# Weighted sums of a graph-attention layer: the product with the coefficients moves from GpSimd to VectorE, and the loads change order

## The reference, cut to what matters

```
x = leaky(x, 0.01) @ W1.T + b1
h = (x @ Wg.T).reshape(N, H, C)
...
coeff = ex / (denom[dst] + 1e-16)
msg = h[src] * coeff[:, :, None]
out = jax.ops.segment_sum(msg, dst, num_segments=N)
out = out.reshape(N, H * C) + bias_g
out = leaky(out, 0.01) @ W2.T + b2
```

## Time and profile before

| | us |
|---|---|
| median of 3 executions | 3251.99 (3251.73 to 3252.8) |
| the profiled execution, its own time | 3261.0 |
| its span, first to last instruction | 3259.2 |
| weighted sums, first load issued to barrier | 1563.3 to 1731.3 |
| busy in the span: TensorE, VectorE, ScalarE, GpSimd | 1741.0, 1931.8, 1077.7, 2424.7 |
| mean granted TensorE clock, share of full speed | 0.671 |

### The profile page before, as it was taken

One profiled execution on the slowest core, in us unless ns is written; L12 is line 12 of the kernel. 1 busy time (PEld: TensorE's weight loads), 2 busy tenths in 40 slices (PEclk: granted clock), 3 DMA queues, 4 the chain that ended last, 5 costly groups with the idle time before them and its releaser, 6 DMA issues.

```text
span 3259.2 us, 39190 instructions
## 1 busy us (share of the span) xinstructions
PE 1741.0 (53%) x7779; PEld 1286.0 (39%) x7779; DVE 1931.8 (59%) x6186; ACT 1077.7 (33%) x2956; POOL 2424.7 (74%) x2038
## 2 busy tenths in 40 slices
PE   1442005888803555563683335667667746555553
PEld 1342004777701222221462334445445535455553
DVE  6984446887813555555896775333333367666664
ACT  1321004665603444442354554222222222212110
POOL 4776787788887777771466775888888878888887
PEclk9665557988956766666555556676676667666666
DMA  8899995455642333331573554565666555555554
GB/s 185 240 311 358 337 354 158 69 61 84 116 36 61 80 79 80 80 79 42 173 217 98 130 131 114 114 116 110 115 114 109 117 124 125 116 114 110 115 114 73
DMA packets 423456, 436.97 MB, mean 134 GB/s; under 512 B 55330, under 2 KB 348883, under 8 KB 423061
## 3 DMA queue, kind: packets, MB, share of 16 engines
q0 software_dynamic: 128576, 130.98, 26.1%
q1 hardware_dynamic: 237472, 240.03, 24.1%
q10 hardware_dynamic: 57336, 65.24, 7.2%
HBM read 248.75 MB, written 187.31 MB: 134 GB/s over the span
## 4 chain that ended last, share of the span: by engine, by line
POOL 29%; issue 12%; DVE 5%; PE 3%; ACT 2%; DMA 1%; ACTq 1%; DVEq 0%; SPq 0%; POOLq 0%
POOL out_dram L718 19%; POOL work L704 11%; DVE work L2103 2%; PE bank L937 1%; ACT work L1322 1%; PE bank L1032 1%; DVE work L1907 1%; PE bank L1110 0%; DMA work<-he,idx_last_s 0%; ACT work L1423 0%; PE bank L1096 0%; DVE work L2140 0%; DVE work L2141 0%; DVE work L2139 0%; DMA work<-s,idx_e_d 0%
## 5 line engine op out<-in xcount | busy, mean ns | idle before, releaser
L1907 DVE TENSOR_TENSOR_SCAN work<-work,bank 128x512 f32<-128x512 bf16 (+1 forms) x294 | 364.1, 1264 | 316.4 <-PE bank L937 292.0
L718 POOL DMA_INDIRECT out_dram<-work,idx_add_s x196 | 313.0, 1597 | 64.7 <-issue 58.5
L718 POOL DMA_INDIRECT out_dram<-big,idx_add_d x196 | 314.8, 1606 | 60.2 <-issue 58.8
L718 POOL DMA_INDIRECT out_dram<-big,idx_add_s x196 | 310.5, 1584 | 61.5 <-issue 54.5
L1315 ACT ACTIVATE work<-work,eps_col 128x4 f32<-128x4 f32 (+1 forms) x196 | 58.5, 299 | 718.0 <-DVE work L1883 717.5
L704 POOL DMA_INDIRECT big<-x_by_edge,idx_e_s x196 | 220.1, 1123 | 75.3 <-issue 59.4
L937 PE MATMUL bank<-ident,work 128*128 128x128 f32 x392 | 106.0, 424 | 298.2 <-ACT work L1322 170.8
L996 PE MATMUL bank<-ident,work 128*128 128x128 f32 x392 | 91.8, 411 | 309.9 <-ACT work L1322 309.9
L1322 ACT ACTIVATE work<-work 128x128 f32<-128x128 f32 x588 | 236.7, 480 | 50.9 <-DVE work L1902 50.9
L704 POOL DMA_INDIRECT work<-he,idx_last_s x196 | 191.4, 977 | 75.5 <-issue 59.4
L704 POOL DMA_INDIRECT work<-d,idx_run_d x196 | 187.6, 957 | 75.4 <-issue 59.4
(11 more groups left out here) (362 smaller groups left out, 5396.7 us busy)
## 6 DMA issues: line engine op xcount, KB each, us to landing
out_dram<-work SPq DMA_DIRECT2D x57, 726.0 KB, 9.0
work<-in_x_dram SPq DMA_DIRECT2D x57, 704.0 KB, 10.1
edge_w<-work SPq DMA_DIRECT2D x49, 512.0 KB
work<-edge_w ACTq DMA_DIRECT2D x49, 512.0 KB, 3.7
work<-flags_src SPq DMA_DIRECT2D x98, 128.0 KB
gat_h<-work SPq DMA_DIRECT2D x49, 256.0 KB
work<-flags_dst SPq DMA_DIRECT2D x98, 128.0 KB
work<-gat_h SPq DMA_DIRECT2D x49, 256.0 KB
```

Of the source, the lines that this page charges most:

```text
L718: g_.indirect_dma_start(table[:, :], bass.IndirectOffsetOnAxis(ap=of[:, at_:at_ + 1], axis=0), row, None, compute_op=ALU.add).then_inc(add ...
L1907: return V.tensor_tensor_scan(to, flag_b[G.place][rows, :], of, before if G.from_(1) else 0.0, ALU.mult, ALU.add)
```

## The change

The GpSimd product and the ScalarE copy before it are taken out. VectorE now multiplies `in_r` by the spread coefficients straight from the PSUM bank. VectorE's body becomes product(G), scan(G-1), leaky(G-2), so scan and leaky each stand one body later than before, and one scan and two leakys follow after the loop. TensorE's spread waits for the product of G-2 (which read its bank) where it waited for the copy. SyncE's order of the three loads becomes coefficients, `gat_h`, flags. The semaphore `coef` is gone.

```diff
             def body(G):
-                load_flags(sp, G, "dst", GATSUM)
+                load_coefficients(sp, G)
                 if G.from_(UNROLL):
                     sp.wait_ge(GATSUM["h"], G.g - (UNROLL - 1))
                     plain(sp)
                 sp.dma_start(in_r[G.place], at(h_dram, G, 512)).then_inc(h_in.of(G), 16)
-                load_coefficients(sp, G)
+                load_flags(sp, G, "dst", GATSUM)
...
-            def products(G):
-                pool.wait_ge(GATSUM["coef"], G.g + 1)
-                h_in.wait(pool, "GATSUM", G)
-                if G.from_(2):
-                    pool.wait_ge(GATSUM["chained"], G.g - 1)
-                g_.tensor_tensor(h_r[G.slot], in_r[G.place], co_r[G.place], ALU.mult).then_inc(GATSUM["h"], 1)
-            for_groups(pool, products)
...
             def spread(G):
                 h_in.wait(pe, "GATSUM", G)
                 if G.from_(2):
-                    pe.wait_ge(GATSUM["coef"], G.g - 1)
+                    pe.wait_ge(GATSUM["h"], G.g - 1)
...
-            def coefficients(G):
-                act.wait_ge(GATSUM["spread"], G.g + 1)
-                if G.from_(UNROLL):
-                    act.wait_ge(GATSUM["h"], G.g - (UNROLL - 1))
-                S_.copy(co_r[G.place], bank[G.slot][:, :]).then_inc(GATSUM["coef"], 1)
-
-            def body(G):
-                coefficients(G)
+            def body(G):
                 if G.from_(2):
                     biased(G.before(2))
...
+            def product(G):
+                dve.wait_ge(GATSUM["spread"], G.g + 1)
+                h_in.wait(dve, "GATSUM", G)
+                if G.from_(2):
+                    dve.wait_ge(GATSUM["chained"], G.g - 1)
+                V.tensor_tensor(h_r[G.slot], in_r[G.place], bank[G.slot][:, :], ALU.mult).then_inc(GATSUM["h"], 1)
+
...
             def body(G):
-                chain_products(G)
+                product(G)
                 if G.from_(1):
-                    leaky(G.before())
+                    chain_products(G.before())
+                if G.from_(2):
+                    leaky(G.before(2))
             for_groups(dve, body)
+            chain_products(group(NG - 1))
+            leaky(group(NG - 2))
             leaky(group(NG - 1))
```

More of the change, by code:

```diff
@@ L333, in build_gnn @@
         MAPS = loop_sems("maps", "step ranked counted signed")
-        GATSUM = loop_sems("gatsum", "spread coef h chained biased z delta kept")
+        GATSUM = loop_sems("gatsum", "spread h chained biased z delta kept")
         HYP = loop_sems("hyp", "var dev taken norm h turned chained he hes")
```

## The result

The changed kernel takes **3229.4 us** (median of 4; 3227.65 to 3234.18) against 3252.4 for the kernel before in the same comparison (median of 4). The ratio is 0.9931, 95% interval 0.9918 to 0.9943, so 23 us or 0.7% are saved (18.5 to 26.7 us by the interval). Forecast were 3225 and a range of 3217 to 3242.

What follows compares the result with a forecast made beforehand. The bound was taken to be VectorE and GpSimd taking turns. With 46 bodies at 2.52 us saving 25.9 us and the tail 1, 27 us off the 3252.0 median gave 3225 us, range 3217 to 3242.

Steps and rivals of the forecast that it cites:

- VectorE's own body: Product 0.60, scan 1.20 and leaky 0.64 on VectorE, neighbours overlapping: 2.44 us; without overlap 2.68 us.
- Rival A: VectorE is the bound but without overlaps: T 2.68 to 2.90 us, kernel 3233 to 3243 us; chance 0.17.
- rival C: Leaky is stretched by something other than GpSimd and stays at 1.69 us: T 3.41, kernel 3266 us; chance 0.01.
- rival D: No change that can be told: T 2.96 to 3.2 us, from several 0.20 us handovers or slightly late loads; chance 0.07.
- Rival B: Slower through late loads, `gat_h` issued after a wait for a scan; at L = 10, 3268 us; chance 0.04.
- the pace: Time per body T in the steady state: between 2.44 and 2.61 us, the middle, 2.52, taken.
- The tail: From leaky(46) to the last delta, the hole between deltas vanishes: 0.8 to 2.6 us saved, 1 taken.
- The clock: TensorE may rise above 1.2 GHz, leaving the loop, T 2.44 us; at the low clock 2.61; rule given half.
- The loop itself: Leaky, delta, spread, product close over two bodies through TensorE: 2.78 + 2.44 = 5.22 us, or 2.61 a body.
- The order on SyncE's queue: Coefficients and `gat_h` queue behind flags(G-1): 4T > 3.8 + L, T above 1.95 us with a 4.0 us landing; covered.
- The copy: Removing ScalarE's copy, 0.59 us a group: worth 0 by itself, bounded by 0 and 0.59 us once.
- The moved steps: VectorE's scan and leaky stand a body later, covering waits on its own work: costed at nothing; 0.20 us each uncovered.

Runs made afterwards that it cites:

- experiment 1: Changed kernel plus a GpSimd 128x512 product per group that nobody reads: body 3.40 us, stage 183.7 us, kernel 3268.6 us in one execution.
- experiment 4: SyncE's loads in the old order, on three kernels: changed kernel, ratio 0.9936; TensorE's spread a group ahead, 0.9945; new order on the kernel before, 0.9988.
- experiment 5: Changed kernel with ScalarE's copy to SBUF put back and VectorE's product reading the copy: body 2.98 us, stage 163.7 us.
- experiment 7: Kernel of experiment 3 with ScalarE's keep of group 45 before biased of group 48 after the loop: ratio 0.9890, stage 139.0 us.
- experiment 6: Changed kernel with VectorE's order product(G), scan(G), leaky(G-1): body 2.617 us, stage 144.7 us; timed, ratio 0.9920.
- experiment 3: Changed kernel with TensorE's spread of group G+1 ahead of delta of G-3, all work kept: ratio 0.9912, body 2.434 us, stage 138.1 us.
- experiment 2: Changed kernel with only the first of delta's four pieces on TensorE: body 2.434 us, stage 137.7 us.

## Why the prediction was right

**Right, shown by runs.** *The bound of before:* the turn with GpSimd (experiment 1). *The size of leaky:* 0.73 where 0.72 was written. *VectorE's product:* 0.687 for 0.68. *VectorE's own body:* 2.434 measured with TensorE out of the way or ahead, 2.44 predicted; so the body of full lengths, 2.68, which the prediction set beside it, is not what these neighbours take. *What is late next:* the spread, by the loop over two bodies that was written out. *Rival A* (no overlaps) is excluded by the distances of starts, *rival C* by experiment 1, and *rival D* by the interval. *Rival B* didn't decide at 2.66 us a body.

**Right in kind, wrong in size.** The step that failed is the pace, "T lies in 2.44 to 2.61, and I take the middle, 2.52". Measured 2.66, outside both ends, which is 46 x 0.14 = 6.4 us. The tail (below) adds 0.9, and the start was 0.6 us shorter than forecast: body 3 began 10.5 us after the first load, where 1574.4 - 1563.3 = 11.1 was put. Together that is the difference between the forecast 27 and the 20.3 us of the stage. The pace has two terms:

- The clock. I gave half a chance to a TensorE at the upper level. The mean over the stage was 0.55, so it had that level for about a tenth of the time, although TensorE was up to 98% busy (9.76 of 10 us above). The seventh stage's rows were no guide to this one. That moves T from 2.52 to 2.59, close to the upper end.
- The loop itself. I closed it as 2.78 + 2.44 = 5.22, and that sum is wrong. 2.44 is the distance from one product to the next; what belongs there is the time from the start of a product to the end of its leaky, 0.60 + 1.20 + 0.72 = 2.52, and 2.52 or 2.53 is what both profiles show in every body. With it my own rows give 5.30, or 2.65 a body. Measured outside the stretches at the upper clock are 5.20 to 5.53, 5.34 on average, or 2.67 a body. So 0.08 of the missing 0.12 is my sum, and 0.04 the handovers, for which 0.22 us a round are left where I had 0.06 + 0.12. That the second round above takes just 5.22 is luck: a handover from spread to product of 0.04 instead of 0.12 makes up for the 0.08.

These handovers differ by the place in the program's loop, which turns every four bodies. From the end of the spread to the product it is 0.23 or 0.24 us in the first body of a turn, 0.19 or 0.20 in the second and 0.04 in the third and fourth, in both profiles and in every turn, but for the stretches at the upper clock and the bodies right behind them. Whether the turn of the loop is the cause wasn't tried.

**Wrong.** *"The order on SyncE's queue ... Covered."* The sum 4T > 3.8 + L was right as a sum for the new order, but it was used only there. The old order was never put through it, and the earlier trace rows gave the landing of a store, 4.0 us, with no word on a load behind two others. The old order costs waits in the changed kernel and 16 us in a faster one (experiment 4). So the change's third part was costed at nothing and has a value, small here.

*The copy.* It was costed at nothing by itself, "bounded by 0 and by 0.59 us once". In the kernel before, the turn with GpSimd sets the pace, and the copy lies beside it. Once the turn is gone the copy would stand in the loop through TensorE, and leaving it out is worth 15.7 us (experiment 5). The sum had no copy in its loop, so the forecast time is not off by this, but a reader of it would take the most valuable part of the change for an idle one.

*The moved steps.* They were costed at nothing, as cover for handovers of 0.20 us. They do hide 0.17 a body, but they also bring leaky closer to the spread that waits for it, and that costs more: 2.617 a body without them, 2.66 with them. The prediction worked out the loop through TensorE and didn't ask whether the old order of steps would have opened it.

*The tail.* One hole was to vanish, between delta 46 and delta 47. It is still there:

```profile
1684.41 2.08 PE L1025 MATMUL bank<-w_W2T,work 128*128 128x128 f32 x8 [0.61 <-DVE work L2096]
...
1685.90 0.72 ACT L1416 ACTIVATE work<-work,cols 128x512 f32<-128x512 f32 x1 [1.43 <-DVE work L1893]
...
1686.53 0.56 ACT L1422 COPY work<-bank 128x512 f32<-128x512 f32 x1
...
1687.24 3.63 PE L1025 MATMUL bank<-w_W2T,work 128*128 128x128 f32 x16 [0.76 <-ACT work L1422]
```

It belongs to ScalarE's order (keep behind biased), as experiment 7 shows, and not to VectorE's. From the end of leaky 46 to the next stage 15.3 us, against 15.4 before: 0.1 us where 1 was put.

The median came out 4 us above the forecast, inside the range and inside the forecast's own case (3219 to 3231). Part of that is luck: the pace of that case, 2.44 to 2.61, was missed, and the stage fell 6.7 us short of the forecast 27. The median came closer because the comparison showed 23 us saved where the stage shows 20.3.

## What to carry to other kernels

An instruction that is recorded longer than its twin elsewhere in the trace, and ends at a fixed distance behind an instruction of another engine, is waiting and not working: look for the twin before costing a move. When a stall is taken out, write out the next loop over all engines and queues and put each part of the change through it, also the orders that it replaces; here a copy on an engine with time to spare, costed at nothing, decides over 15.7 of 20.3 us, and an order of three loads that was worth nothing at 3.07 us a body is worth 2 us at 2.66 and 16 at 2.43. In such a loop count each engine's share from the start of its first step to the end of its last, and not from one body to the next. And a step put off to hide a handover may close a loop elsewhere sooner: 0.17 us hidden, 0.22 lost.

## What the runs showed of the hardware that was not expected

**The clock does not follow the busy share in the records.** With the scan in the same body (experiment 6) TensorE was busy for 98.98 of 100 us and its granted clock was 0.50 throughout. With the spread ahead (experiment 3) it was busy for 84.66 and the clock was 0.71:

```profile
1575.00:1675.00 100.00, 98.98 (x344) 71.63 (x344) 96.56 (x116) 46.06 (x78) 0.00 (x0) 0.50 0.85 254
```

```profile
1575.00:1675.00 100.00, 84.66 (x370) 62.02 (x369) 100.00 (x124) 52.66 (x82) 0.00 (x0) 0.71 0.89 275
```

The matrix work is the same in both, in another order and at another pace. What in it keeps the clock down in the first is not shown by these runs; a kernel's clock could not be read off its busy share here.

**Lengths on VectorE are no distances.** In experiment 2 product, scan and leaky are recorded at 0.75, 1.35 and 0.79 us, in the changed kernel at 0.69, 1.28 and 0.73. The distances of their starts are the same wherever nothing is waited for, 0.60, 1.19 and 0.64. The sum of lengths would be 2.89 us a body where 2.43 was measured.
